# Attention block on one core: row maxima turned by a float32 transpose in place of a float32 matmul

## The chip, the cores and the metric

The kernel runs on one core of a Trainium2 chip. The metric is the device time of one execution in microseconds (us); the median of several runs is compared. PE is TensorE, the matrix engine (PEld its weight loads), ACT is ScalarE, DVE is VectorE, POOL is GpSimd, and SP is SyncE, which issues the DMAs here.

## What is computed

```python
xs = reshape(gn(x), (16, 1024, 512))          # gn: group norm over 32 groups, float32
q, k, v = (einsum('btc,hcd->bhtd', xs, W) for W in (Wq, Wk, Wv))   # 8 heads of 64
att = softmax(einsum('bhtd,bhsd->bhts', q, k) / 8)
out = einsum('bhts,bhsd->bhtd', att, v)       # back to (16, 1024, 512)
return x + reshape(out @ Wproj + bproj, x.shape)
```

## The kernel before

The work goes batch by batch (16) and head by head (8); a head is a *step* of 16 *slots* (BLOCKS). A slot handles one block: 128 keys by 512 queries of a head. On PE, slot i issues the scores of block i + 3 (two matmuls, L571 and L572), then the product of block i with the values (PV, three matmuls L690 to L692, since every operand is split into a high and a low part), and then the slot's *other work*: row scores of the next head (L578), from which DVE takes row maxima (L864), and the entries of a table WORK. An entry is a piece of work that leaves its result in one of two PSUM banks in turn, each freed when DVE has read it: "qk" and "qn" (query and key projections of a coming head, L517), "v" (values), "xt" (four transposes of a normalised token tile by `nc.tensor.transpose`, L549), "mean" and "var" (float32 matmuls with a group-averaging matrix, L553 and L555), "proj" (output projection, L561), and "mt", the subject here.

ACT takes the exponential of each score block twice (L710, prob and prob_h) and copies finished PV accumulators out (L781, acc). The difference prob_l is made by POOL (L1031) for 11 of a head's 16 blocks and by DVE (L803) for the others. A "mt" entry runs once per half head. Its input is nmax, 128 partitions by 8, the negated row maxima (L869); it turns four of these columns into four rows of 128, which DVE copies out (L875) and an SP DMA lays into row 64 of q_lm, where the second score matmul (L572) uses them to subtract each query's maximum. The table puts "mt" mostly in slots 1 and 10:

```python
"plain": ((1, "mt", 1, 0, 1), (10, "mt", 0, 0, 1), (10, "qn", 0, 0, 3), (12, "qn", 1, 0, 3), ...
"tokens": ((0, "xt", 0, 0, 4), (1, "mt", 1, 0, 1), (2, "xt", 1, 0, 4), ...      # head 6
"next": ((0, "mt", 1, 0, 1), (1, "xt", 5, 0, 4), ...                             # head 7
"proj": (... (8, "proj", 4, 0, 4), (9, "mt", 0, 0, 1), (10, "proj", 5, 0, 4), ...  # head 0 of the next batch
```

The order on each engine is written out by hand, and every hand-over is a semaphore. The head steps of kinds "tokens", "next" and "proj" occur once in each of 15 batches. The mt matmul's operands are plain float32, while L517, L571, L572, L578 and L690 to L692 use float32r, a form that takes one pass.

Of the kernel before, what the change touches and what calls it, by code (L numbers as in the profile page):

```python
# [1 line left out]

# [9 lines left out]
P = 128  # L26
# [6 lines left out]
BLOCKS = 16  # L33
AHEAD = 3
POOL_BLOCKS = (1, 4, 5, 6, 7, 8, 9, 11, 12, 13, 15)

WORK = {
# [84 lines left out]
class Plan:  # L137


    def __init__(self, batches):  # L140
        self.prologue = [("mean", 0), ("var", 0)] + [("xt", t) for t in range(4)]
        self.prologue += [("mean", 1), ("var", 1)] + [("xt", t) for t in range(4, 8)]
        self.prologue += [("qk", 0), ("qk", 1), ("qn", 0), ("qn", 1), ("v", 0), ("v", 1), ("mt", 0), ("v", 2), ("v", 3)]
        self.place = {("start", 0, e): n for n, e in enumerate(self.prologue)}
        n = len(self.prologue)
        self.steps = {}
        for section, ks in (("first", [0]), ("body", range(1, 9)), ("last", range(1, 8))):
            if section == "last":
                n = body_start + self.per_batch * (batches - 1)
            if section == "body":  # L150
                body_start = n
            for k in ks:
                has_next = section != "last"
                slots = fillers(k % 8, has_next, k == 8)
                assert not slots[BLOCKS - 1]
                ends = []
                for s, slot in enumerate(slots):


                    for kind, a, lo, hi in slot:  # L160
                        if lo == 0:
                            assert len(ends) < 2 or ends[-2] < s
                            ends.append(BLOCKS)
                        if hi == CHUNKS[kind]:
                            ends[-1] = s
                self.steps[section, k] = slots
                for s in slots:
                    for kind, a, lo, hi in s:
                        if lo == 0:
                            self.place[section, k, (kind, a)] = n  # L170
                            n += 1
            if section == "body":
                self.per_batch = n - body_start
        for t in range(8):
            self.place["last", 8, ("proj", t)] = n + t
        assert self.per_batch % 2 == 0


class Step:

    def __init__(self, eng, it, section, k, plan, last_batch, bases):
        self.eng, self.it, self.section, self.k = eng, it, section, k
        self.plan, self.bases = plan, bases
# [37 lines left out]
def attention_block(nc, x, Wq, Wk, Wv, Wproj, bproj, out):  # L223
# [15 lines left out]
    with ExitStack() as ctx:  # L239
        def sb(name, shape, dt=F32):  # L240
            return ctx.enter_context(nc.sbuf_tensor(name, shape, dt))

        def sem(name):
            return ctx.enter_context(nc.semaphore(name))
# [8 lines left out]
        ident = sb("ident", [P, P])  # L253
# [1 line left out]

        xh = sb("xh", [P, CH, T], F32R)
        xl = sb("xl", [P, CH, T], F32R)

        VW = 2 * D + 1
# [18 lines left out]
        nmax = sb("nmax", [P, TT])  # L280
# [37 lines left out]
        mt_done = sem("mt_done")  # L318
# [59 lines left out]
                step(Step(eng, B - 1, "last", k, plan, B, None))  # L378

        def ring3(s, i):  # L380

            return (BLOCKS * s.h + i) % (BLOCKS * NH) % 3
# [128 lines left out]
        def _(pe):  # L513
            def split_product(bank, cols, pairs, start, stop):
                n = len(pairs)
                for j, (w, m) in enumerate(pairs):
                    last = nc.tensor.matmul(ps[bank][:, cols], w, m, start=start and j == 0,  # L517
                                            stop=stop and j == n - 1)
                return last

            def entry(kind, a, lo, hi, bank, before, head, wait):

                w = ps[WB + bank]
                if lo == 0 and before is not None:
                    pe.wait_ge(taken[bank], before)
                wait()
                if kind in ("qk", "qn"):
                    cols = slice(a * 512, (a + 1) * 512)
                    for c in range(lo, hi):
                        last = split_product(WB + bank, slice(0, 512),  # L530
                                             [(wqk_h[:, c, head, :], xh[:, c, cols]),
                                              (wqk_l[:, c, head, :], xh[:, c, cols]),
                                              (wqk_h[:, c, head, :], xl[:, c, cols])], c == 0, c == CH - 1)
                    if hi == CH:
                        last.then_inc(qk_done, 1)
                elif kind == "v":
                    half, e = divmod(a, 4)
                    vcols = slice(half * 256, (half + 1) * 256)
                    for j in range(2):
                        t = slice((2 * e + j) * P, (2 * e + j + 1) * P)  # L540
                        for c in range(CH):
                            last = split_product(WB + bank, slice(j * 256, (j + 1) * 256),
                                                 [(xh[:, c, t], wv_h[:, c, vcols]),
                                                  (xh[:, c, t], wv_l[:, c, vcols]),
                                                  (xl[:, c, t], wv_h[:, c, vcols])], c == 0, c == CH - 1)
                    last.then_inc(v_done, 1)
                elif kind == "xt":
                    for c in range(CH):
                        last = nc.tensor.transpose(w[:, c * P:(c + 1) * P], xs[:, a % 4, c * P:(c + 1) * P],  # L549
                                                   ident[:, :])  # L550
                    last.then_inc(xt_done, 1)
                elif kind == "mean":
                    nc.tensor.matmul(w[:, 0:4], group_avg[:, :], mv[:, :, 0], start=True, stop=True).then_inc(mean_done, 1)  # L553
                elif kind == "var":
                    nc.tensor.matmul(w[:, 0:4], group_avg[:, :], spread[:, :], start=True, stop=True).then_inc(var_done, 1)  # L555
                elif kind == "mt":
                    nc.tensor.matmul(w[0:4, 0:P], nmax[:, a * 4:(a + 1) * 4], ident[:, :],
                                     start=True, stop=True).then_inc(mt_done, 1)
                elif kind == "proj":
                    for c in range(CH):  # L560
                        last = nc.tensor.matmul(w[:, :], o[:, c, a * P:(a + 1) * P], wp[:, c, :],  # L561
                                                start=c == 0, stop=c == CH - 1)
                    last.then_inc(proj_done, 1)
# [21 lines left out]
            def start_entry(kind, a, h=0, wait=nothing):  # L585
                pos = plan.place["start", 0, (kind, a)]
                before = pos // 2 if pos >= 2 else None
                entry(kind, a, 0, 4 if kind in ("qk", "qn", "v", "xt") else 1, pos % 2, before, h, wait)
# [66 lines left out]
            def step(s):  # L655
                first = s.section == "first"
                end = s.h == 7 and not s.has_next
                for i in range(BLOCKS):

                    ahead, j = divmod(i + AHEAD, BLOCKS)  # L660
                    if not (end and ahead):
                        def wait():
                            pe.wait_ge(prob_h_ready, s.heads(BLOCKS, 0, i + 1 + early(s, i)))
                            if j == 0:
                                pe.wait_ge(mrow_in[0], s.heads(16, 1, 16))
                            if j == TT:
                                pe.wait_ge(mrow_in[1], s.heads(16, 0, 16))
                        scores((s.k + ahead) % 2, j, ring3(s, i + AHEAD), wait)
# [8 lines left out]
                    if tc == 0 and t % 2 == 0 and s.h in (0, 4):  # L677
# [5 lines left out]
                        else:  # L683
                            entry_taken(pe, s, "v", 4 + t // 2, back=3 - t // 4)
                    lo_wait(pe, s, i)
                    ring = ring3(s, i)
                    c0 = 0 if s.h % 2 == 0 else 1
                    v_hi_op, v_lo_op = vh[:, t, pair, c0:c0 + P], vl[:, t, pair, c0:c0 + P]
# [11 lines left out]
            for t in range(TT):  # L700
                bk, before = s.bank("proj", t)
                entry("proj", t, 0, 4, bk, before, 0, nothing)
# [399 lines left out]
```

## Time and profile before

| | |
|---|---|
| median of 3 runs | 4950.16 us (4949.59 to 4951.74) |
| span of the profiled execution | 4946.9 us |
| PE busy | 4705.1 us, 95% |
| PEld busy | 3505.4 us, 71% |
| ACT busy | 2886.6 us, 58% |
| DVE busy | 2775.5 us, 56% |
| POOL busy | 2326.6 us, 47% |

The span runs from the first instruction's start to the last one's end; the median lies 3.3 us above it. Busy times are unions of the records' durations, and matmul records overlap, because a matmul starts before the one ahead of it has left the array. What a matmul costs PE is therefore read from start to start in the timeline and not from its duration.

### The profile page before, as it was taken

How to read it: one execution, taken by the hardware profiler on the slowest of the kernel's cores; microseconds unless marked ns; L12 is line 12 of the kernel's file. 1: busy time of each engine (PE TensorE's matmuls, PEld its weight loads, DVE VectorE, ACT ScalarE, POOL GpSimd, SP SyncE). 2: the span in 40 equal slices, each digit the busy share in tenths (PEclk: the TensorE clock that was granted, in tenths of full speed). 3: DMA queues.
4: the chain of work that ended last, by engine and by line, in shares of the span. 5: the costliest groups of instructions: out<-in, count | busy, mean ns of one | idle time of the engine just before them, and what ended most of it. 6: DMA issues, size and time to landing. Idle time of an engine off the chain costs nothing.

```text
span 4946.9 us, 73065 instructions
## 1 busy us (share of the span) xinstructions
PE 4705.1 (95%) x20608; PEld 3505.4 (71%) x20608; DVE 2775.5 (56%) x5284; ACT 2886.6 (58%) x5507; POOL 2326.6 (47%) x1837
## 2 busy tenths in 40 slices
PE   7999999999999999999999999999999999999998
PEld 5777767777676776767767677676776767767675
DVE  5655646556465564655646556465564655646454
ACT  4665646556465564655646566464664646656465
POOL 2444545445454454544545445454444545445455
PEclk9999999999999999999999999999999999999999
DMA  2111111111111111111111111211112111111101
GB/s 69 34 37 55 31 53 35 46 46 32 52 34 50 43 34 54 31 53 41 32 54 35 51 41 30 63 28 53 37 30 62 35 49 35 32 61 34 53 23 51
DMA packets 156934, 212.71 MB, mean 43 GB/s; under 512 B 56544, under 2 KB 57568, under 8 KB 156512
## 3 DMA queue, kind: packets, MB, share of 16 engines
q1 hardware_dynamic: 156512, 207.47, 15.0%
q8 instruction: 218, 3.57, 0.3%
q14 instruction: 204, 1.67, 0.1%
HBM read 105.12 MB, written 34.08 MB: 28 GB/s over the span
## 4 chain that ended last, share of the span: by engine, by line
issue 50%; POOL 42%; PE 6%; POOLq 1%; ACT 1%; DVE 0%; DMA 0%; SPq 0%; ACTq 0%; DVEq 0%
POOL prob_l L1031 32%; POOL o L1048 6%; POOL res L1054 3%; PE bank L517 1%; PE bank L561 1%; POOLq L1030 1%; POOL rstd L1023 1%; PE bank L578 1%; PE bank L690 1%; PE bank L692 1%; PE bank L691 1%; PE bank L571 0%; PE bank L572 0%; POOLq L1047 0%; DMA xs<-in_x 0%
## 5 line engine op out<-in xcount | busy, mean ns | idle before, releaser
L1031 POOL TENSOR_TENSOR prob_l<-prob,prob_h 128x512 fp32r<-128x512 f32 x1408 | 1803.5, 1288 | 2470.5 <-ACT prob_h L710 2452.6
L710 ACT ACTIVATE prob<-bank 128x512 f32<-128x512 f32 x2048 | 1237.6, 604 | 1698.6 <-PE bank L572 1579.3
L864 DVE TENSOR_REDUCE smax<-bank 128x1 f32<-128x512 f32 x2048 | 1349.1, 684 | 1012.6 <-PE bank L578 997.8
L710 ACT ACTIVATE prob_h<-bank 128x512 fp32r<-128x512 f32 x2048 | 1236.7, 604 | 198.6 <-PE bank L692 154.9
L690 PE MATMUL bank<-prob_h,vh 128*128 128x512 f32 x2048 | 832.6, 407 | 117.9 <-ACT acc L781 99.3
L578 PE MATMUL bank<-k_hl,q_hh 128*128 128x512 f32 x2048 | 802.5, 436 | 33.6 <-DVE smax L864 30.4
L571 PE MATMUL bank<-q_hh,k_hl 128*128 128x512 f32 x2048 | 824.0, 402 | 0.5 <-ACT prob_h L710 0.5
L572 PE MATMUL bank<-q_lm,k_h 65*128 65x512 f32 x2048 | 813.8, 397 | 0.0
L692 PE MATMUL bank<-prob_l,vh 128*128 128x512 f32 x2048 | 809.6, 395 | 0.0
L691 PE MATMUL bank<-prob_h,vl 128*128 128x512 f32 x2048 | 809.0, 395 | 0.0
L803 DVE TENSOR_TENSOR prob_l<-prob,prob_h 128x512 fp32r<-128x512 f32 x640 | 508.0, 804 | 511.9 <-ACT prob_h L710 511.8
L690 PEld LDWEIGHTS bank<-prob_h,vh 128*128 128x128 f32 x2048 | 389.8, 190 | 272.7 <-issue 166.5
L578 PEld LDWEIGHTS bank<-k_hl,q_hh 128*128 128x128 f32 x2048 | 374.0, 189 | 206.8 <-DVE smax L864 92.2
L561 PE MATMUL bank<-wp,o 128*128 128x512 f32 x1024 | 462.2, 595 | 22.0 <-DVE res L997 11.9
L571 PEld LDWEIGHTS bank<-q_hh,k_hl 128*128 128x128 f32 x2048 | 387.0, 189 | 103.3 <-issue 35.8
L691 PEld LDWEIGHTS bank<-prob_h,vl 128*128 128x128 f32 x2048 | 390.4, 191 | 90.2 <-issue 8.7
L692 PEld LDWEIGHTS bank<-prob_l,vh 128*128 128x128 f32 x2048 | 386.4, 189 | 90.4
L572 PEld LDWEIGHTS bank<-q_lm,k_h 65*128 65x128 f32 x2048 | 386.4, 189 | 84.7 <-issue 3.6
L517 PE MATMUL bank<-xh,wqk_h 128*128 128x512 f32 x1024 | 407.7, 398 | 0.0
L517 PE MATMUL bank<-xl,wqk_h 128*128 128x512 f32 x1024 | 400.3, 391 | 0.0
L517 PE MATMUL bank<-xh,wqk_l 128*128 128x512 f32 x1024 | 399.4, 390 | 0.0
L1048 POOL TENSOR_TENSOR o<-acc,inv_b 64x512 f32<-64x512 f32 x256 | 331.1, 1293 | 100.8 <-DMA inv_b<-inv_dram 61.6
(58 smaller groups left out, 4393.2 us busy)
## 6 DMA issues: line engine op xcount, KB each, us to landing
xs<-in_x SPq DMA_DIRECT2D x128, 256.0 KB, 2.8
q_hh<-q_hh SPq DMA_DIRECT2D x256, 128.0 KB, 2.2
k_hl<-k_h SPq DMA_DIRECT2D x256, 128.0 KB, 2.4
inv_b<-inv_dram SPq DMA_DIRECT2D x256, 128.0 KB, 2.8
res<-in_x SPq DMA_DIRECT2D x128, 256.0 KB, 2.7
out_x<-res SPq DMA_DIRECT2D x128, 256.0 KB, 2.0
q_lm<-q_lm SPq DMA_DIRECT2D x256, 2.0 KB
den<-acc SPq DMA_DIRECT2D x256, 2.0 KB, 1.7
```

The lines of the kernel that those rows point to most:

```text
L517: last = nc.tensor.matmul(ps[bank][:, cols], w, m, start=start and j == 0, stop=stop and j == n - 1)
L561: last = nc.tensor.matmul(w[:, :], o[:, c, a * P:(a + 1) * P], wp[:, c, :], start=c == 0, stop=c == CH - 1)
L571: nc.tensor.matmul(s_bank[:, :], k_hl[:, slot, keys], q_hh[:, slot, queries], start=True, stop=False)
L572: nc.tensor.matmul(s_bank[:, :], k_h1[0:D + 1, slot, keys], q_lm[0:D + 1, slot, queries], start=False, stop=True).then_inc(scores_ready, 1)
L578: nc.tensor.matmul(ps[SM + j % 2][:, :], q_hh[:, slot, t * P:(t + 1) * P], k_hl[:, slot, half * 512:(half + 1) * 512], start=True, stop=Tr ...
L690: nc.tensor.matmul(ps[bank][:, :], v_hi_op, prob_h[:, ring, :], start=t == 0, stop=False)
L691: nc.tensor.matmul(ps[bank][:, :], v_lo_op, prob_h[:, ring, :], start=False, stop=False)
L692: nc.tensor.matmul(ps[bank][:, :], v_hi_op, prob_l[:, ring, :], start=False, stop=t == TT - 1).then_inc(pv_done, 1)
L710: return nc.scalar.activation(out, ps[ST + bank][:, :], ACT.Exp, scale=SCALE)
L864: nc.vector.tensor_reduce(smax[:, j:j + 1], ps[SM + j % 2][:, :], AX.X, ALU.max).then_inc(rows_used, 1)
L1031: nc.gpsimd.tensor_tensor(prob_l[:, r3, :], prob[:, ring2, :], prob_h[:, r3, :].bitcast(F32), ALU.subtract).then_inc(prob_l_pool, 1)
L1048: nc.gpsimd.tensor_tensor(o[r, h // 2, tc * 512:(tc + 1) * 512], acc[r, tc, :], inv_b[r, :], ALU.mult).then_inc(o_ready, 1)
```

## The change

The mt entry is issued as a transpose by the identity (transpose mode) in place of a matmul with the identity. Input, output, bank, semaphore and place in the order stay as they are. The rest of the diff removes empty lines, so line numbers move.

```diff
                 elif kind == "mt":
-                    nc.tensor.matmul(w[0:4, 0:P], nmax[:, a * 4:(a + 1) * 4], ident[:, :],
-                                     start=True, stop=True).then_inc(mt_done, 1)
+                    nc.tensor.transpose(w[0:4, 0:P], nmax[:, a * 4:(a + 1) * 4], ident[:, :]).then_inc(mt_done, 1)
```

## Rows read from the trace of the kernel before

**Rows 1.** The page: span, busy time of PE.
```profile
span 4946.9 us, 73065 instructions
PE 4705.1 (95%) x20608; PEld 3505.4 (71%) x20608; DVE 2775.5 (56%) x5284; ACT 2886.6 (58%) x5507; POOL 2326.6 (47%) x1837
```
**Rows 2.** Who waited for whom: us in total, times, longest us.
```profile
ACT prob L710 <- PE bank L572: 1579.3, 1069, 4.7
```
**Rows 3.** The mt line: duration ns min/median/max, starts, form; who waited.
```profile
L557 PE MATMUL bank<-ident,nmax x512: 272/273/421, 61.0 to 4886.3; 128*4 128x128 f32 x171
...
  DVE q_lm L875: 41.5, 91
```
**Rows 4.** Timeline, PE around one mt: start us, us, instruction, count.
```profile
1979.34 0.40 PE L692 MATMUL bank<-prob_l,vh 128*128 128x512 f32 x1
1979.67 0.38 PE L557 MATMUL bank<-ident,nmax 128*4 128x128 f32 x2
1979.98 0.50 PE L571 MATMUL bank<-q_hh,k_hl 128*128 128x512 f32 x1
1980.32 0.40 PE L572 MATMUL bank<-q_lm,k_h 65*128 65x512 f32 x1
1980.55 0.40 PE L690 MATMUL bank<-prob_h,vh 128*128 128x512 f32 x1
```
**Rows 5.** The same mt's weight loads; in brackets the idle time before.
```profile
1979.66 0.09 PEld L557 LDWEIGHTS bank<-ident,nmax 128*4 128x4 f32 x2 [0.36 <-issue]
```
**Rows 6.** Timeline, PE around four transposes of x.
```profile
2117.27 0.39 PE L692 MATMUL bank<-prob_l,vh 128*128 128x512 f32 x1
2117.50 0.60 PE L549 MATMUL bank<-ident,xs 128*128 128x128 f32 x4
2117.86 0.48 PE L578 MATMUL bank<-k_hl,q_hh 128*128 128x512 f32 x1
2118.17 0.40 PE L571 MATMUL bank<-q_hh,k_hl 128*128 128x512 f32 x1
```
**Rows 7.** Timeline, PE around a group-mean matmul (two L578 stand between).
```profile
2022.87 0.40 PE L692 MATMUL bank<-prob_l,vh 128*128 128x512 f32 x1
2023.10 0.28 PE L553 MATMUL bank<-mv,group_avg 128*128 128x4 f32 x2
...
2023.79 0.40 PE L571 MATMUL bank<-q_hh,k_hl 128*128 128x512 f32 x1
```
**Rows 8.** Timeline, projection head, slots 9 and 10: PE, DVE, POOL.
```profile
1917.10 1.55 PE L561 MATMUL bank<-wp,o 128*128 128x512 f32 x3 [0.80 <-DVE res L997]
...
1916.35 0.69 DVE L997 TENSOR_TENSOR res<-bank,res 128x512 f32<-128x512 f32 x1 [3.31 <-POOL res L1054]
...
1913.72 1.28 POOL L1031 TENSOR_TENSOR prob_l<-prob,prob_h 128x512 fp32r<-128x512 f32 x1 [6.12 <-ACT prob_h L710]
```
**Rows 9.** Timeline, head 6, slots 1 and 2: PE, DVE, ACT.
```profile
2112.39 0.54 PE L549 MATMUL bank<-ident,xs 128*128 128x128 f32 x3 [0.67 <-DVE xl L841]
...
2111.57 0.69 DVE L841 TENSOR_TENSOR xl<-bank,xh 128x512 fp32r<-128x512 f32 x1 [1.03 <-ACT xh L717]
...
2109.97 0.60 ACT L710 ACTIVATE prob<-bank 128x512 f32<-128x512 f32 x1 [0.68 <-DVE prob_l L803]
```
**Rows 10.** Timeline, head 7, slot 1: PE and DVE.
```profile
2139.59 0.66 PE L549 MATMUL bank<-ident,xs 128*128 128x128 f32 x4
...
2138.78 0.68 DVE L841 TENSOR_TENSOR xl<-bank,xh 128x512 fp32r<-128x512 f32 x1
```
**Rows 11.** PE's waits in one batch (1905 to 2215 us): total, times, longest.
```profile
PE bank L690 <- ACT acc L781: 6.9, 7, 1.8
```
**Rows 12.** Windows: length, busy us (count) by engine, PEclk, DMA share, GB/s.
```profile
60.00:4910.00 4850.00, 4642.78 (x20400) 3467.25 (x20399) 2734.44 (x5207) 2869.18 (x5480) 2310.11 (x1813) 1.00 0.15 42
353.83:357.24 3.41, 3.41 (x9) 2.20 (x9) 2.64 (x4) 1.89 (x4) 1.33 (x2) 0.50 0.45 156
...
4637.56:4640.97 3.41, 3.41 (x10) 1.95 (x9) 2.24 (x4) 1.79 (x3) 1.37 (x2) 0.50 0.40 123
```

## The prediction, made before the change was run

> **What bounds the kernel now.** I read the views in this order: the page's totals and clock, who waits for whom, then the timeline of TensorE (PE) around the changed instruction. PE is busy for 4705.1 of 4946.9 us and each other engine for at most 58% [rows 1]; its granted clock between 60 and 4910 us has the mean 1.00, the full 2.4 GHz [rows 12]. The largest waits of ScalarE (ACT) are for PE's score matmuls [rows 2]. So PE sets the pace, and time taken from its queue comes off the span, except where a stall right behind the saving is ended by an engine that did not get earlier.
>
> **What the changed entry costs PE.** The kernel has one "mt" entry per half head: 2 halves x 8 heads x 16 batches = 256. Each is now two LDWEIGHTS/MATMUL pairs, 512 records of a 128x4 stationary tile and 128 streamed columns [rows 3]. Durations of pipelined matmuls overlap, so I count from start to start. Two full matmuls with nothing between them follow each other at 0.23 us (1980.32 to 1980.55) [rows 4]. Around an mt the starts are: the last PV matmul 1979.34, first pass 1979.67, the next real matmul 1979.98, the one after it 1980.32 [rows 4]. That is 0.98 us for what takes 2 x 0.23 = 0.46 us without the entry: an mt costs PE 0.52 us. Its parts: 0.33 before the first pass; 0.11 from the first to the second (the merged row lasts 0.38 and one pass 0.27 [rows 3, 4]); 0.20 from there to the next matmul, since 0.31 lies between the rows; 0.34 for that matmul, which should take 0.23. The weight load of an mt isn't pulled under the matmul before it: the load path idles 0.36 us first [rows 5].
>
> **What the new entry costs.** The trace has no transpose of 4 columns. The nearest rows are the four one-pass transposes of x, same float32 identity, same 128 streamed columns, but a 128x128 stationary tile: previous matmul 2117.27, transposes 2117.50 (x4, together 0.60 us), next matmul 2117.86, the one after it 2118.17 [rows 6]. The first starts a normal 0.23 us behind its predecessor. The merged row exceeds one pass of 0.27 by 0.33, so each further transpose adds 0.11. Taking three off, one transpose would need 0.23 + 0.03 + 0.31 = 0.57 us where the mt needs 0.98. By rows rounded to 0.01 that saves 0.41; I take 0.40. Of it 0.11 is the second pass; the other 0.3 is the late start before the entry and the late start behind it.
>
> Does the 0.3 belong to the second pass or to the 4-column tile? The rows can say: the group-mean matmul is also plain float32 and two passes, but its stationary tile is 128x128. It starts 0.23 us behind its predecessor (2022.87 to 2023.10), not 0.33, and from there to 2023.79 there is one ordinary matmul extra; 0.92 - 3 x 0.23 = 0.23 us for both passes [rows 7]. So plain float32 alone doesn't cause the late start; the 128x4 shape does, as if the array were emptied before it and again after it.
>
> The Trainium skill, page "TensorEngine Tiling (Array Packing)", section "Key Properties", says that changing the tiling mode drains the engine. Its section "Restrictions" says that column tiling rules out the transpose mode for float32. By the first rule the 0.33 against 0.23 of these rows is such a drain, and they agree; by the second a float32 transpose would have to use the full array, which no run here shows yet, and the drain would go.
>
> I take the full-array case, whose price the transpose rows give: 0.12 us, saving 0.40. Its bounds: the two-pass full-array rows at 0.23 for the entry, a saving of 0.29 [rows 7]; at the other end the entry at 0.12, since a 4-column load is not seen to be dearer than a 128-column one. If the shape alone keeps the late starts, only 0.11 goes (rival A).
>
> **What becomes of each saving.** Nothing is added: no wait, no DMA, no instruction on another engine. The result is read by VectorE's copy, then SyncE (SP) moves it into the query tile. VectorE waits for it 41.5 us in 91 times [rows 3], which can only shrink; the copy, SP's DMA and the score matmul behind them come earlier with it. I followed PE's stalls through one whole batch and looked at what ends each. At a head's first PV matmul PE waits for ACT's copy of the accumulator, 7 times in this batch for 6.9 us in all [rows 11]; that copy waits for PE's own last matmul, so the stall moves with PE and takes nothing. At three places the stall's end is anchored ahead of the mt:
> - the projection step: PE waits for 0.80 us until 1917.10, right behind the slot of an mt, for VectorE's output addition of 1916.35, which was released by GpSimd's bias addition, which GpSimd had queued behind the prob_l it began at 1913.72, before that mt [rows 8];
> - head 6: the second token transpose starts at 2112.39, behind VectorE's xl of 2111.57, behind ACT, which was itself late on VectorE's prob_l at 2109.97 [rows 9];
> - head 7: the transpose at 2139.59 waits for the bank that the xl of 2138.78 frees, work of the step before the mt [rows 10].
>
> Each of these occurs once in 15 of the 16 batches: 45 of 256 savings end in a longer stall. The other 211 count. Later stalls on maxima and norms in heads 3 and 6 are ended by VectorE work that itself waited for PE behind the mt, so I let those move.
>
> **Sum.** 211 x 0.40 = 84.4 us. Span 4946.9 - 84.4 = 4862.5; the median before lies 3.3 us above the profiled span (4950.16), so 4865.8 us.
>
> Another term is left at zero: PE's clock. It falls to half (1.2 GHz) for 3.41 us at a time at the end of ACT's longest copy wait (1.8 us, the step into the projection head), at 10 of the 15 boundaries (the first and the last of the ten are shown); during one, PE starts 9 or 10 matmuls where 3.41 / 0.23 would be 15, at half rate, so it costs 3.41 / 2 = 1.7 us, 17 us for ten [rows 11, 12]. Which boundaries are hit may shift once the batch is 5 us shorter: between 17 us less and 5 x 1.7 = 9 us more. The forecast's own range: all 256 savings count, 102 us, gives 4848, which I round up to 4850; 211 x 0.29 = 61 us gives 4889.
>
> **The rivals.**
> - A, the late starts stay. If they hang on the 4 columns and not on a tiling mode that a transpose can't use, only the second pass goes: 211 x 0.11 = 23 us, 4927. For it: the shape stays 128x4, and nothing in the trace shows a 4-column transpose. Against it: the transposes of x start on time in front and behind [rows 6]. 13%.
> - B, other engines take half. The savings of slot 1 come right behind the head's ACT wait, where ACT has a copy and four exponentials to catch up; if it then holds PE back, the slot 1 savings go as well, 6 counted ones x 16 batches x 0.40 = 38 us: 4904. For it: ACT and VectorE are late in head 6 at that place [rows 9]. Against: ACT's waits behind are for PE [rows 2]. 7%.
> - C, still two passes: the instruction is lowered as before and nothing happens, 4950. Against: the transposes of x are one record each, x4 for four [rows 6]. 2%.
> - D, slower, through the clock. The fall to 1.2 GHz follows a stretch in which PE stood still for 1.8 us. If the thinner work of slot 1 let it fall behind the shorter waits too, at each of the other 118 head starts, at 1.7 us each [rows 12], that is 200 us more: 4950 - 84 + 200 = 5066. It decides from 84 / 1.7 = 50 extra falls. Against: only the 1.8 us wait brings one now, the others none, and the transposes of x run with the matmuls around them at their 0.23 us [rows 6]. 3%.
>
> The Trainium skill, page "TensorE: Matmul & The Clock Gate", section "Part 4: PE-mode transpose", says that work in transpose mode doesn't count toward the full clock as matmuls do; that speaks for D, and by it the 256 entries would cease to hold the clock. The token transposes in the trace show no such loss.
>
> **How the numbers follow.** Forecast 75%, A 13%, B 7%, D 3%, C 2%. The forecast with B holds 82%, so the range runs from 4850 to B's end with a little room, 4906. A measurement of this kernel tells about 0.2%, or 10 us, from no change. Forecast, A (0.46%) and B are faster: 0.95. C is the same: 0.02. D is slower: 0.03.
>
> **What the profile after would show.** One LDWEIGHTS/MATMUL pair per entry, 256 records. For the forecast: the load starts under the previous matmul, the transpose 0.23 us behind it, and the second matmul behind it 0.57 us after the last PV matmul. For A: 0.33 us before it, and 0.87 in all. The projection stall on res should be 0.4 us longer than 0.80, those on xl as well. The copy wait of each head should be as it is; if it grows by 0.4, B is right. PEclk tells D at a glance. The forecast is wrong if the transpose's start to start is dear for a reason that neither shape shows, or if more of the stalls are anchored ahead of an mt than the three I found in one batch.

## The result

The changed kernel takes 4860.26 us (4858.98 to 4860.77, 4 runs) against 4950.95 us (4949.59 to 4955.44, 4 runs) of the kernel before: a ratio of 0.9816, interval 0.9802 to 0.983. It is 91 us faster; 4865.8 us was predicted. The page of the profile after, to set beside [rows 1]:

```profile
span 4858.9 us, 72553 instructions
PE 4610.2 (95%) x20352; PEld 3496.1 (72%) x20352; DVE 2775.0 (57%) x5284; ACT 2864.6 (59%) x5507; POOL 2319.6 (48%) x1837
```

PE has 256 matmuls and 256 weight loads fewer and is as full as it was. The mt line, which has become L526 (for [rows 3]), and the timeline around one entry, for [rows 4]:

```profile
L526 PE MATMUL bank<-ident,nmax x256: 270/271/415, 61.2 to 4797.8; 128*4 128x128 f32 x128
...
  DVE q_lm L843: 22.3, 82
```

```profile
1944.97 0.40 PE L660 MATMUL bank<-prob_l,vh 128*128 128x512 f32 x1
1945.20 0.27 PE L526 MATMUL bank<-ident,nmax 128*4 128x128 f32 x1
1945.23 0.48 PE L539 MATMUL bank<-q_hh,k_hl 128*128 128x512 f32 x1
1945.54 0.40 PE L540 MATMUL bank<-q_lm,k_h 65*128 65x512 f32 x1
```

From the last PV matmul to the second matmul behind the entry it is 0.57 us now (1944.97 to 1945.54), where it was 0.98. Part by part, in the medians: 0.09 us are saved before the entry, 0.28 from the entry to the next matmul (the second pass of 0.11, and 0.17 of late start), and 0.02 for that matmul, which takes 0.31 to 0.32 us here where it took 0.34. The transpose starts 0.23 us behind its predecessor although its tile is still 128x4. Its weight load, for [rows 5], runs under that matmul, with no idle time before it:

```profile
1944.97 0.08 PEld L526 LDWEIGHTS bank<-ident,nmax 128*4 128x4 f32 x1
```

**Where the time went.** PE executes the same sequence in both traces if the two passes of an old entry count as one. So each start-to-start interval can be subtracted from its twin. The first instruction's offset aside, these differences add up to 87.8 us, and by place they are:

| place | us |
|---|---|
| around the mt entries, outside half clock (0.40 each at most places) | +85.7 |
| given back: projection head, slot 10 | -6.0 |
| given back: head 6, slot 2 | -5.7 |
| given back: head 7, slot 12 | -3.5 |
| given back: head 3, slots 3 and 4 | -2.3 |
| intervals touched by half clock in either trace (12 mt entries among them) | +15.7 |
| restart of the batch loop on PE (head 1, slots 0 and 1) | +4.4 |
| all others | -0.5 |

The first give-back is the stall of [rows 8]. After the change it reads:

```profile
1880.72 1.29 POOL L999 TENSOR_TENSOR prob_l<-prob,prob_h 128x512 fp32r<-128x512 f32 x1 [6.10 <-ACT prob_h L678]
...
1883.35 0.69 DVE L965 TENSOR_TENSOR res<-bank,res 128x512 f32<-128x512 f32 x1 [3.31 <-POOL res L1022]
...
1884.10 0.70 PE L529 MATMUL bank<-wp,o 128*128 128x512 f32 x1 [1.18 <-DVE res L965]
```

PE waits 1.18 us where it waited 0.80: the 0.4 us won by the mt just before it. In head 6, PE waits for xl 1.07 us where it was 0.67 [rows 9]:

```profile
2075.05 0.65 PE L518 MATMUL bank<-ident,xs 128*128 128x128 f32 x4 [1.07 <-DVE xl L809]
```

Three further places lose their saving otherwise; for each, rows of after follow below. At the start of head 7 the mt stands right in front of the PV matmul that waits for ACT's copy, so the entry was hidden in both kernels. In head 7's slot 11 the mt itself waits for nmax, for 0.18 us in both kernels, and what it saves is lost one slot later: the projection there starts right behind DVE's vl (2136.48 + 0.89), whose read frees its bank, 0.53 us behind the last PV matmul where it was 0.29. In head 3's slot 1 the next row score starts 0.20 us behind the transpose and not 0.03, with the weight path idle before it; the profile names nothing that released it:

```profile
2099.33 0.27 PE L526 MATMUL bank<-ident,nmax 128*4 128x128 f32 x1
2099.77 0.50 PE L658 MATMUL bank<-prob_h,vh 128*128 128x512 f32 x1 [0.17 <-ACT acc L749]
```

```profile
2135.33 0.27 PE L526 MATMUL bank<-ident,nmax 128*4 128x128 f32 x1 [0.18 <-DVE nmax L837]
...
2136.90 0.40 PE L660 MATMUL bank<-prob_l,vh 128*128 128x512 f32 x1
2137.43 0.50 PE L486 MATMUL bank<-xh,wqk_h 128*128 128x512 f32 x1
...
2136.48 0.89 DVE L825 TENSOR_TENSOR vl<-bank,vh 128x128 fp32r<-128x128 f32 x4
```

```profile
1980.61 0.30 PEld L546 LDWEIGHTS bank<-k_hl,q_hh 128*128 128x128 f32 x2 [0.34 <-issue]
```

The clock part: the trace before has 10 stretches of 3.41 us at half clock at head 0 [rows 12], the trace after has 3. Windows over the whole and over the first and last of the three:

```profile
60.00:4810.00 4750.00, 4542.65 (x20127) 3454.75 (x20128) 2733.46 (x5205) 2843.63 (x5474) 2298.26 (x1810) 1.00 0.15 42
348.36:351.78 3.42, 3.42 (x11) 2.43 (x10) 2.56 (x4) 2.04 (x4) 1.24 (x1) 0.50 0.49 152
...
4253.21:4256.62 3.41, 3.41 (x10) 2.42 (x10) 2.58 (x4) 1.85 (x4) 1.30 (x2) 0.50 0.56 153
```

After the change a batch takes 301.67 us on average with such a fall and 300.17 without: a fall costs 1.5 us. The wait of PE for the accumulator copy ahead of it is 1.76 to 1.78 us in both kernels, in all 15 batches. So the wait didn't change; how often it brought a fall did.

### The profile page after: what moved, and what is told of

Read it like the earlier page. It is cut to its first block, busy times and chain, and to the rows that moved or that the text cites. A ratio compares the mean times of both kernels' runs of the same rounds, so it can differ in the third digit from the quotient of the medians.

```text
span 4858.9 us, 72553 instructions
## 1 busy us (share of the span) xinstructions
PE 4610.2 (95%) x20352; PEld 3496.1 (72%) x20352; DVE 2775.0 (57%) x5284; ACT 2864.6 (59%) x5507; POOL 2319.6 (48%) x1837
## 4 chain that ended last, share of the span: by engine, by line
issue 50%; POOL 42%; PE 6%; POOLq 1%; ACT 1%; DVE 1%; DMA 0%; SPq 0%; ACTq 0%; DVEq 0%
POOL prob_l L999 32%; POOL o L1016 6%; POOL res L1022 3%; PE bank L486 1%; PE bank L529 1%; POOL rstd L991 1%; POOLq L998 1%; PE bank L546 1%; PE bank L658 1%; PE bank L660 1%; PE bank L659 1%; PE bank L540 0%; PE bank L539 0%; POOLq L1015 0%; ACT prob_h L678 0%
## 5 line engine op out<-in xcount | busy, mean ns | idle before, releaser
L529 PE MATMUL bank<-wp,o 128*128 128x512 f32 x1024 | 462.9, 596 | 27.7 <-DVE res L965 17.8
```

## The experiments

What was left open was what the 0.3 us of late starts hang on, whether the give-backs are understood, and what the clock has to do with the change. Times are medians; "falls" are the stretches of 3.41 us at half clock between 100 and 4750 us of the span, from the records of the granted clock of the one profiled execution of each kernel. The count isn't the same in every execution: e5's profiled one had 4 falls at a mean granted clock of 0.997, two of its other three runs show 0.995. So the counts below belong to the traces, and the medians beside them to four or five runs.

### One price for the tile, one for the pass

**e1_mm128.** Two float32 passes, but 128 stationary columns; the identity and the averaging matrix move into one tile with the maxima (the cut shows the entry alone):

```diff
-nc.tensor.transpose(w[0:4, 0:P], nmax[:, a * 4:(a + 1) * 4], ident[:, :])
+nc.tensor.matmul(w[:, 0:P], mixed[:, a * (P + 4):a * (P + 4) + P], ident[:, :], start=True, stop=True)
```

> The mt entry is a plain float32 matmul again, in two passes, but with a stationary tile of 128 columns: its four columns of maxima and 124 of a constant matrix beside them; rows 0 to 3 of the result are read as before. Theory (the late starts of the old entry came from its four-column tile): no late start, 0.23 us from the last PV matmul to the first pass, and some 0.69 us from that PV matmul to the second matmul behind the entry, where the transpose has 0.57 and the old entry 0.98; the time is about 0.12 x 190 = 22 us above the changed kernel, 4882 us. Rival (the late starts belong to two-pass matmuls in this place): 0.33 us before it and 0.98 in all, 4950 us.

```profile
1964.06 0.39 PE L660 MATMUL bank<-prob_l,vh 128*128 128x512 f32 x1
1964.28 0.38 PE L525 MATMUL bank<-mixed 128*128 128x128 f32 x2
1964.42 0.48 PE L539 MATMUL bank<-q_hh,k_hl 128*128 128x512 f32 x1
1964.74 0.40 PE L540 MATMUL bank<-q_lm,k_h 65*128 65x512 f32 x1
```

The entry behaves as the theory says: 0.22 us before it and 0.68 us in all (the median is 0.69). The late starts are gone with both passes in place. These passes stream 128 columns, as the mt did; the group-mean matmul of [rows 7] streamed only 4, and both cost the same 0.23 us. The time, 4906.02 us (4905.04 to 4909.58), 0.9915 of the kernel before, is 24 us above the forecast. Taken apart in the way of the table above, its intervals add up to 48.7 us more than the changed kernel's (the medians differ by 45.8): 24.2 us around the entries, of which some 5 are given back, so this term came near the theory's 22; 15.2 us in intervals with half clock (12 falls against 3); 6.6 us at the restart of the batch loop; and 7.6 us elsewhere, most of it in the query and key projections, whose matmuls start some 0.005 us further apart. Whether the moved tiles cause the last wasn't tried.

**e2_bf16_mm4 and e3_bf16_tr4.** One pass, four columns, in bfloat16, as a matmul and in transpose mode (ident_bf16 is the upper half of each float32 word of the identity):

```diff
-nmax = sb("nmax", [P, TT])
+nmax = sb("nmax", [P, TT], BF16)
-nc.tensor.transpose(w[0:4, 0:P], nmax[:, a * 4:(a + 1) * 4], ident[:, :])
+nc.tensor.matmul(w[0:4, 0:P], nmax[:, a * 4:(a + 1) * 4], ident_bf16, start=True, stop=True)      # e2
+nc.tensor.transpose(w.bitcast(BF16)[0:4, 0:P], nmax[:, a * 4:(a + 1) * 4], ident_bf16)            # e3
```

> The maxima are written as bfloat16 (what is subtracted in the exponent is rounded, so the output differs in its last digits), and the mt entry is a bfloat16 matmul with the identity: one pass, four columns. Theory (four-column tile): the late starts stay, 0.33 us before it and 0.87 in all; only the second pass is gone, 0.11 x 190 = 21 us below the kernel before, 4929 us. Rival (one pass is what counts): 0.57 us in all and 4860 us, as the changed kernel.

> As the bfloat16 matmul of four columns, but in transpose mode, with a bfloat16 result. It tells transpose mode from tile. Theory (tile: only a float32 transpose is forced onto the full array): as the bfloat16 matmul, 0.33 us before it, 0.87 in all, 4929 us. Rival (transpose mode by itself spares the late starts): 0.57 in all, 4860 us.

```profile
1968.81 0.40 PE L662 MATMUL bank<-prob_l,vh 128*128 128x512 f32 x1
1969.13 0.22 PE L527 MATMUL bank<-ident,nmax 128*4 128x128 bf16 x1
1969.28 0.50 PE L541 MATMUL bank<-q_hh,k_hl 128*128 128x512 f32 x1
1969.62 0.40 PE L542 MATMUL bank<-q_lm,k_h 65*128 65x512 f32 x1
```

```profile
1968.45 0.40 PE L661 MATMUL bank<-prob_l,vh 128*128 128x512 f32 x1
1968.77 0.22 PE L527 MATMUL bank<-ident,nmax 128*4 128x128 bf16 x1
1968.92 0.50 PE L540 MATMUL bank<-q_hh,k_hl 128*128 128x512 f32 x1
1969.26 0.40 PE L541 MATMUL bank<-q_lm,k_h 65*128 65x512 f32 x1
```

Both keep the late starts: 0.32 us before the entry (0.33 in the median) where e1 has 0.23, and 0.15 us from the pass to the next matmul where e1 and the transpose have 0.03, 0.81 us in all. Both take 4914.4 us, 0.9932 of before. One pass alone is therefore worth little, and transpose mode by itself nothing: the bfloat16 transpose costs what the bfloat16 matmul costs. It came out at 0.81 us and not 0.87, since the short bfloat16 pass lets the next matmul start after 0.15 us and not 0.20. The times lie 34 us below the kernel before in the same session (4948.05), where 21 was expected: 36.8 us around the entries, some 8 us of it given back, 4.5 us at the restart. Together with e1: a four-column stationary tile brings the late starts, except in a float32 transpose. By the rule cited ahead, from the Trainium skill, page "TensorEngine Tiling (Array Packing)", section "Restrictions", that one can't be column-tiled; what the four kernels show agrees with it, though no record names the tile.

**e4_twice.** Each transpose issued twice:

```diff
+nc.tensor.transpose(w[0:4, 0:P], nmax[:, a * 4:(a + 1) * 4], ident[:, :])
 nc.tensor.transpose(w[0:4, 0:P], nmax[:, a * 4:(a + 1) * 4], ident[:, :]).then_inc(mt_done, 1)
```

> The changed kernel with each float32 transpose of the maxima issued twice (the same result written twice). Theory: a transpose costs PE 0.11 us, and it is added at some 190 of 256 places, where no wait hides it: 0.11 x 190 = 21 us more, 4881 us. Rival (a four-column transpose is cheaper than the 0.11 of the 128-column ones, since its weights are 4 columns): 0.05 x 190 = 10 us more, 4870 us.

```profile
1956.91 0.27 PE L526 MATMUL bank<-ident,nmax 128*4 128x128 f32 x1
1957.02 0.27 PE L527 MATMUL bank<-ident,nmax 128*4 128x128 f32 x1
```

The second one comes 0.11 us behind the first, so a 4-column transpose costs what a 128-column one does, and the rival falls. The time is 4899.66 us, 39 us above the changed kernel and not 21. Subtracted interval by interval: 22.1 us around the entries, of which 4 us are given back, but 15.2 us in intervals with half clock (11 falls, two of them at restarts of the loop) and 5.8 us at the loop's restart. The price was right and the sum again missed the clock and the restart.

### Taking away what swallows a saving

**e5_bias_before and e6_bias_after.** GpSimd adds one bias ahead of its prob_l, in the kernel before and in the changed one:

```diff
+if s.section == "body" and s.k == 8 and i == 8:
+    add_bias(s, PROJ_SLOTS.index(i))
 if j in POOL_BLOCKS and not (end and ahead):
     lo_part(j % 2, ring3(s, i + AHEAD), s.heads(BLOCKS, ahead, j + 1))
...
-if i == at:
+if i == at and i != 8:
     add_bias(s, t)
```

> The kernel before with one move: in slot 8 of the projection head GpSimd adds the bias to the residual tile before its prob_l and not after it. Theory: the wait of 0.80 us at the fifth-to-sixth projection entry, which VectorE's output addition ends, was anchored at that prob_l, ahead of the mt of slot 9; without it the 1.05 us that the spot loses in each of 15 batches go, 16 us, 4932 us. Rival (something else holds the bank, such as the load of the residual tile): nothing, 4948 us.

> The changed kernel with the same move on GpSimd. Theory: there the spot loses 1.45 us, since it swallowed the 0.40 us that the mt of slot 9 saved; all of it goes, 22 us, 4838 us, and the mt change is worth 6 us more on top of this move than without it, in the intervals outside half clock. Rival: nothing, 4860 us. What neither says is the clock: falls may be 3 or some 11, up to 14 us on top.

The stall vanishes; in e6 the eight passes of the projection follow the PV matmul at once:

```profile
1881.73 0.40 PE L660 MATMUL bank<-prob_l,vh 128*128 128x512 f32 x1
1881.97 3.60 PE L529 MATMUL bank<-wp,o 128*128 128x512 f32 x8
```

At this place e5 wins 15.8 us over the kernel before and e6 wins 21.8 us over the changed one, as the two theories' 16 and 22 said: the 6 us of difference are the saving that the stall had swallowed. The times tell another story. e5 takes 4926.56 us, 25 us less than the kernel before in the same session (4951.55): between the two traces 15.8 us are the stall and 10.2 lie in intervals with half clock (4 falls and not 10), less 3.4 at the restart. e6 takes 4856.76 us, only 3.5 us less than the changed kernel: it has a fall in every one of its 15 batches, which takes 17.8 us back. The first of them, in the timeline; from 347.20 on, matmuls start 0.42 to 0.43 us apart:

```profile
346.68 0.72 PE L658 MATMUL bank<-prob_h,vh 128*128 128x512 f32 x1 [1.78 <-ACT acc L749]
347.20 0.63 PE L659 MATMUL bank<-prob_h,vl 128*128 128x512 f32 x1
347.62 0.63 PE L660 MATMUL bank<-prob_l,vh 128*128 128x512 f32 x1
348.05 0.63 PE L539 MATMUL bank<-q_hh,k_hl 128*128 128x512 f32 x1
```

### The clock

**e7_nudge1 and e8_nudge4.** One and four more transposes per batch:

```diff
+if a == 0 and head in (3,):            # e8: (2, 3, 5, 6)
+    nc.tensor.transpose(w[0:4, 0:P], nmax[:, a * 4:(a + 1) * 4], ident[:, :])
```

> The changed kernel with one more transpose per batch (the mt in slot 10 of head 2 is issued twice): 16 x 0.11 = 2 us of work. Theory (the number of falls to half clock depends on how the batch's length falls, and not on how long the waits are): the falls at head 0 may go from 3 to about 10, each 1.5 to 1.7 us, and the time rises by more than its work, to between 4862 and 4874 us, with the rise over 2 us in proportion to the falls counted. Rival (the clock follows what the mt entry itself is): 3 falls, 4862 us.

> The same with four more transposes per batch (heads 1, 2, 4 and 5): 64 x 0.11 = 7 us of work. Theory: 4867 us plus 1.5 to 1.7 us for each fall above 3, so up to 4881 us. Rival: 3 falls, 4867 us.

e7 takes 4860.56 us with 1 fall and e8 4869.01 us with 4. In e7 the 2 us of work were repaid by two falls fewer; in e8, 7.2 us are work and 1.9 us half clock (its profiled execution is the slowest of its four; the intervals add up to 11.6 us, 2.5 of them in small pieces). The theory's large swing didn't come at these two lengths, and the rival's constant 3 didn't either. That the falls don't hang on the mt entry stands on e5 against the kernel before (the same entry, 4 falls and 10) and e6 against the changed kernel (15 and 3). I have no rule by which a kernel's count could be told beforehand: in order of batch length without falls, 300.2, 300.3, 300.8, 301.8, 302.2, 302.8, 302.8, 304.2 and 305.0 us had 3, 1, 4, 11, 12, 11, 11, 4 and 10 falls, and e6, whose batches all had one, lasted 300.3 us each.

**e9_late and e10_late_bias.** A projection of head 7 moves behind the accumulator copy, without and with the bias move:

```diff
-    ... (12, "qn", 0, 0, 4), (13, "qn", 1, 0, 4)),     # "next", head 7
+    ... (12, "qn", 0, 0, 4), (14, "qn", 1, 0, 4)),
-    "proj": (0, 1, 1, 1, 2, 0, 1, 2, 1, 2, 1, 1, 1, 1, 1, 0),
+    "proj": (0, 0, 2, 1, 2, 0, 1, 2, 1, 2, 1, 1, 1, 1, 1, 0),
```

> The changed kernel with the second query/key projection of head 7 moved from slot 13 to slot 14, so that ScalarE copies it out after the accumulator and not before it, and the first row score of the projection head moved from slot 1 to slot 2. Theory (the falls to half clock hang on PE's 1.76 us wait for that accumulator copy, the longest of a batch): the wait shrinks to about the 0.3 to 0.8 us of other heads, 1 to 1.4 us in each of 15 batches, and the falls end: 15 to 21 us and 3 x 1.5 = 5 us less, 4834 to 4840 us. Rival (the wait is moved on, to the row scores, whose doubled halves come by DMA 2.4 us after the copy): nothing won, 4860 us, and the falls stay or grow.

> The same with the bias move on GpSimd. Theory: no falls, so the bias move brings its full 22 us here, of which the falls took 18 before: 4812 to 4818 us. Rival (each batch gets its fall whatever the wait): 15 x 1.5 = 22 us above that.

```profile
2152.69 0.49 PE L658 MATMUL bank<-prob_h,vh 128*128 128x512 f32 x1 [1.26 <-ACT acc L749]
...
2157.24 0.73 PE L546 MATMUL bank<-k_hl,q_hh 128*128 128x512 f32 x2 [1.16 <-DMA k_hl<-k_h]
```

Both theory and rival were half right. The wait shrank from 1.76 to 1.26 us only, yet no fall is left, in 15 boundaries each of e9 and e10. But the wait came back in slot 2 for the DMA that doubles the keys' low part, as the rival said. e9 takes 4868.75 us, 8 us more than the changed kernel, where its theory had 4834 to 4840. e10 takes 4846.39 us, 22 us less than e9, so here the bias move brings all it wins, but from e9's higher time it ends 28 us above its theory's 4812 to 4818.

**e11_best and e12_best_old_mt.** e10 with the row scores of the projection head begun in slot 3, and its twin with the old mt entry:

```diff
-    "proj": (0, 0, 2, 1, 2, 0, 1, 2, 1, 2, 1, 1, 1, 1, 1, 0),
+    "proj": (0, 0, 0, 2, 2, 2, 1, 1, 1, 2, 1, 1, 1, 1, 1, 0),
```

> The kernel with both moves (late projection of head 7, bias first) in which the first row scores of the projection head go from slot 2 to slot 3. Theory: in it PE waited 1.16 us (1.6 us with the slower restart) in slot 2 for the DMA that doubles the keys' low part; one slot with a projection later that wait is gone, 1.3 to 1.6 us in each of 15 batches, 20 to 24 us below 4846: 4822 to 4827 us, without falls at head 0. Rival (another engine holds PE there as well, VectorE's maxima above all): less than half of it, 4836 us or more.

> The same kernel with the old mt entry, a float32 matmul of two passes. It measures the change where the clock doesn't fall and the projection stall doesn't swallow a saving. Theory: 256 entries of 0.40 us, less the three places per batch at which the trace of the changed kernel shows the saving lost (head 7 at both of its mt entries, head 6 in slot 1; 45 in all) and most of those in slot 1 of head 3 (13 of 16): 198 x 0.40 = 79 us above its twin. Rival (the clock's share of the difference belongs to the mt entry and comes in any kernel): 88 us or more.

e11 takes 4826.81 us (4825.23 to 4827.85), 0.9744 of the kernel before (0.9731 to 0.9758) and 33 us below the changed kernel, within its theory's 4822 to 4827. It has no fall:

```profile
60.00:4780.00 4720.00, 4537.66 (x20140) 3454.92 (x20141) 2716.19 (x5207) 2844.23 (x5479) 2309.19 (x1811) 1.00 0.15 43
```

e12 takes 4913.48 us, 87 us above its twin, which looks like the rival's number. By intervals, though, it is 89.4 us around the entries less 11.3 us given back, so 78 us where the theory had 79; 1.9 us of half clock (one fall, at a restart, where PE had waited 1.66 us; none at head 0); and 6.6 us at the restart of the loop. So the change's own worth is 78 us in a kernel without falls, and the remaining 7 us again come with the restart.

## Why the prediction was right, and where it wasn't

**The price of the entry: right.** From 0.98 to 0.57 us, both read off before. The step that carried it was to ask, by the group-mean rows [rows 7], whether two passes or four columns cause the late starts. e1 shows that they go with the tile while both passes stay, and e2 and e3 that they stay while one pass goes. One part of the 0.52 us was laid to the wrong cause: the matmul behind the entry "which should take 0.23" takes 0.31 to 0.32 also behind the transpose and in e1, so of its 0.34 only 0.02 is a late start. The total wasn't touched by it, since the price of the transpose was taken from [rows 6], where the same 0.31 stands. Rival A was a real case: the bfloat16 form of the same change is worth 34 us and not 91. Rival C is out by the 256 records.

**211 counted savings: too many.** In intervals outside half clock 85.7 - 17.5 us remain, and with the 12 entries inside it (4.8 us) 73.0 us: 183 savings of 0.40. The projection head and head 6 came as told, 6.0 and 5.7 us. For head 7's first mt the loss was right and the place wrong: it was not the bank of the transpose at [rows 10] but ACT's copy, right behind the entry. That should have been read from the order of the slots: a wait that moves with PE takes nothing from a saving ahead of it, unless the entry stands between PE's last PV matmul, for which the copy waits, and the matmul that waits for the copy. The sentence that such stalls "take nothing" missed that case. Two places I didn't have, head 7's slot 11 and head 3's slot 1. At the first PE ran close behind DVE's vl without standing still, so the list of stalls of before had no row for it; at the second the cause isn't shown. The term was 84.4 us and is 73.0.

**The clock, left at zero: the term that made up for it.** Ten falls became three: 15.7 us in all, of which 4.8 belong to the entries, so 10.9 us. It lay within the bounds given (17 us less to 9 us more). That the time came within 6 us of the forecast is the meeting of a sum 11 us too high and a clock that gave 11 us, with 4 us more from the loop's restart. In e6, with 15 falls and not 10, the same term would have cost some 8 us, at 1.5 us each.

**Rival B** is seen in small, in head 3's slot 1, where the time behind the entry grows by 0.17 us; the waits for the copy are equal within 0.01 us at the starts of heads 0 and 2 to 6, and those of heads 1 and 7 differ for the reasons given. **Rival D** is wrong in its link: the falls came behind PE's waits of 1.76 to 1.78 us at head 0 and, four times (e1, e4 twice, e12), behind a wait of 1.66 to 1.70 us at a restart of the loop; none came behind the 1.26 us of e9 to e12, and the transposes in the slots of a head start brought none. The passage on transpose mode in the Trainium skill, page "TensorE: Matmul & The Clock Gate", section "Part 4: PE-mode transpose", is not seen at work here: with 256 more transposes the kernel had fewer falls, though so few and short ones can't test it.

**Left open.** Why the restart of the batch loop is cheaper with one-pass entries. The first PV matmul of head 1 waits for the same copy in both kernels; in the kernel before it starts later, by a varying amount. For each kernel, before first, the matmul and its weight load:

```profile
1941.70 0.39 PE L690 MATMUL bank<-prob_h,vh 128*128 128x512 f32 x1 [1.14 <-ACT acc L781]
1940.84 0.19 PEld L690 LDWEIGHTS bank<-prob_h,vh 128*128 128x128 f32 x1 [0.72 <-issue]
```

```profile
1907.84 0.50 PE L658 MATMUL bank<-prob_h,vh 128*128 128x512 f32 x1 [0.29 <-ACT acc L749]
1907.83 0.19 PEld L658 LDWEIGHTS bank<-prob_h,vh 128*128 128x128 f32 x1 [0.72 <-issue]
```

The copy ends 1.02 us after the start of the last PV matmul ahead of it in both, and the weight load starts behind it in both; it is the matmul that comes 0.86 us after its own weights. From the first PV matmul of the projection head's last slot to this one it is 1.61 us at each of the 14 restarts in all the kernels with one instruction pair per entry (e2, e3, e6 to e11 too), and 2.44 to 2.68 us on average in all with two (before, e1, e4, e5, e12). Part of it reappears a few matmuls later. So it goes with the number of instructions in the loop's body and not with the kind of entry: e4 has transposes and pays, e2 has a matmul and doesn't.

The traces hold one candidate, the transfers of kind "instruction" on queue q8, 16 KB each:

```profile
q8 instruction: 218, 3.57, 0.3%
```

One of them ends near each restart. In the 70 restarts of the five kernels with two pairs, the late matmul starts 1.1 to 1.7 us after that end, and the two times rise and fall together (correlation 0.92). In the nine kernels with one pair the transfer ends in the same stretch and the matmul takes no notice. This fits PE waiting for the next piece of its program between the weight load and the matmul. No run moves the program without changing the work, so it isn't shown.

## What to carry to other kernels

A small float32 matmul among large ones can cost several times its own passes, if the shape of its stationary tile makes the matmuls around it start late: read start to start from the matmul before it to the second behind it, and ask of rows of other shapes whether the pass or the tile is to blame. A saving on the bounding engine counts at each place until that engine next waits for something that didn't move, so walk one period of the schedule place by place, near misses too. And in a kernel whose clock falls after a long wait, compare versions with the falls counted and set apart: a move worth 22 us showed as 3.5 us until the wait that brought the falls was shortened.

## What was not expected of the hardware

- The same wait of 1.76 to 1.78 us in every batch brought between 1 and 15 falls to half clock per kernel (3 in the changed one, 10 before, 15 in e6, each in one trace), each about 1.5 us of time, and the 1.45 us per batch that the bias move takes off were enough to go from 3 to 15; with the wait at 1.26 us there was none in the 60 boundaries of e9 to e12.
- A bfloat16 transpose of four columns keeps the late starts (0.81 us), while a float32 one has none (0.57 us): the wider type is the cheaper one here.
- At the restart of a loop PE's next PV matmul came 0.83 to 1.07 us later in the programs with 16 matmuls more per batch, of some 1280; with what reappears behind it, 0.3 to 0.6 us per restart. With 4 matmuls more (e8) it came no later.
